# Adaptive condition and a feed-forward layer: the second half's condition product moved between the steps of the first group

## The reference

```python
W = weights[condition]                       # 32 of 16 matrices of 64 x 64, chosen by itok
y = einsum('bct,bcd->bdt', x, W)             # x: (32, 64, 1024)
h = gelu(einsum('bsd,df->bsf', y, inter_w) + inter_b, approximate=True)   # 1024 -> 4096
out = x + einsum('bsf,fd->bsd', h, output_w) + output_b                   # 4096 -> 1024
```

## Time and profile before

| | us |
|---|---|
| median of 3 runs (1282.69 to 1284.75) | 1283.48 |
| the profiled execution | 1285.43 |
| its span in the profile | 1282.4 |
| TensorE busy in it | 1258.2 |
| VectorE / ScalarE / GpSimd busy | 825.2 / 561.8 / 194.9 |
| granted TensorE clock, mean | 0.995 |

### The profile page before, as it was taken

How to read it: one execution, slowest core, us unless ns; L and a number is a source line. 1 busy time by engine, 2 the same in 40 slices (tenths; PEclk the granted TensorE clock), 3 DMA queues, 4 the chain that set the end, 5 groups by cost and what they waited for, 6 DMA issues and landing times.

```text
span 1282.4 us, 15344 instructions
## 1 busy us (share of the span) xinstructions
PE 1258.2 (98%) x5634; PEld 1043.3 (81%) x5634; DVE 825.2 (64%) x1078; ACT 561.8 (44%) x949; POOL 194.9 (15%) x105
## 2 busy tenths in 40 slices
PE   7799999999999999999999999999999999999998
PEld 7678888878888888888888888888888888888886
DVE  3857676877477677847665555554547767784764
ACT  3445544544454444444434444444445444444442
POOL 4623331223000000000033333222300000000000
PEclk9899999999999999999999999999999999999999
DMA  9625667654899433228735345443289942233431
GB/s 353 237 89 194 258 236 274 229 200 178 298 393 353 154 99 99 99 99 355 290 141 187 126 180 181 181 153 105 120 296 395 351 155 99 99 99 99 159 125 45
DMA packets 88601, 249.50 MB, mean 195 GB/s; under 512 B 8114, under 2 KB 8146, under 8 KB 87122
## 3 DMA queue, kind: packets, MB, share of 16 engines
q1 hardware_dynamic: 87442, 248.27, 53.3%
q10 hardware_dynamic: 1088, 0.28, 0.1%
HBM read 162.55 MB, written 85.98 MB: 194 GB/s over the span
## 4 chain that ended last, share of the span: by engine, by line
PE 91%; DVE 5%; DMA 3%; issue 1%; ACT 0%; SPq 0%; POOLq 0%; DVEq 0%; POOL 0%
PE ps L516 48%; PE ps L500 42%; DVE lhs L719 1%; PE ps L463 1%; DVE y L711 1%; DMA y_in<-y_raw_mem 1%; DMA h_mem<-c 1%; DMA y_raw_mem<-y_stage 1%; DVE y_whole L714 1%; DVE y_out L821 0%; DMA cond_all<-in_L_cond_weights_dram 0%; DVE y_stage L706 0%; DVE hs L733 0%; DVE y_whole L706 0%; DVE c L726 0%
## 5 line engine op out<-in xcount | busy, mean ns | idle before, releaser
L500 PE MATMUL ps<-y,lhs 128*128 128x512 f32 x2688 | 616.5, 391 | 10.5 <-DVE lhs L719 7.3
L516 PE MATMUL ps<-rhs,lhs 128*128 128x512 f32 x2688 | 609.6, 389 | 0.0
L500 PEld LDWEIGHTS ps<-y,lhs 128*128 128x128 f32 x2688 | 507.1, 189 | 119.5 <-issue 6.4
L516 PEld LDWEIGHTS ps<-rhs,lhs 128*128 128x128 f32 x2688 | 504.5, 188 | 104.8
L640 ACT ACTIVATE lhs<-h_raw 128x512 fp32r<-128x512 f32 x224 | 141.6, 632 | 345.8 <-PE ps L516 340.1
L778 DVE TENSOR_TENSOR lhs<-h_raw,lhs 128x512 fp32r<-128x512 f32 x224 | 155.1, 692 | 188.4 <-ACT lhs L640 188.4
L719 DVE TENSOR_TENSOR lhs<-w_raw,lhs 128x512 fp32r<-128x512 f32 x128 | 106.3, 831 | 132.1 <-ACT lhs L570 132.0
L719 DVE TENSOR_TENSOR lhs<-s_w,lhs 128x512 fp32r<-128x512 f32 x96 | 99.3, 1035 | 89.4 <-ACT lhs L570 89.3
L570 ACT ACTIVATE lhs<-w_raw 128x512 fp32r<-128x512 f32 x128 | 80.7, 632 | 172.1 <-PE ps L500 168.4
L781 DVE TENSOR_TENSOR rhs<-W,rhs 128x512 fp32r<-128x512 f32 x224 | 153.5, 685 | 0.0
L436 POOL TENSOR_TENSOR s_w<-w_raw 128x1024 f32<-128x1024 f32 x16 | 48.7, 3045 | 627.9 <-PE ps L516 354.6
(11 more groups left out here) (31 smaller groups left out, 287.7 us busy)
## 6 DMA issues: line engine op xcount, KB each, us to landing
h_raw<-h_mem SPq DMA_DIRECT2D x112, 512.0 KB, 3.4
w_raw<-in_L_ffn_inter_w_dram SPq DMA_DIRECT2D x32, 1024.0 KB, 9.0
h_mem<-hs SPq DMA_DIRECT2D x64, 512.0 KB, 4.9
W<-in_L_ffn_output_w_dram SPq DMA_DIRECT2D x32, 1024.0 KB, 12.7
h_mem<-c SPq DMA_DIRECT2D x48, 512.0 KB, 5.8
y_mem<-y_out SPq DMA_DIRECT2D x28, 512.0 KB, 3.1
y<-y_mem SPq DMA_DIRECT2D x7, 2048.0 KB, 13.6
x<-in_x_dram SPq DMA_DIRECT2D x16, 512.0 KB, 11.4
```

The lines of the kernel that those rows point to most:

```text
L500: last = nc.tensor.matmul(ps[:, bank, :], w[:, k, :], y[i][:, part, k, :], start=(i in FRESH and k == 0 and u == 0), stop=(k == KH - 1 and ...
L516: last = nc.tensor.matmul(ps[:, bank2(h, j, tb), :], lhs[s % RING][:, a, blk(tb)], rhs[r][:, w, :], start=(j in FRESH and q == 0 and u == ...
```

## The change

For the first pass `cond` is as before, tile by tile; its evictions are `y_keep`, `y_high`, `y_low` and `y_sum` work on halves of 1024 columns with a semaphore each, and steps 0 and 1 wait for the banks and halves that they use. The picks for these tiles are shared: GpSimd, ScalarE and VectorE each take every third, unrolled. The product of a tile of the second pass is a call of its own, `cond1(j)`. It writes two of the banks 4 to 7, and TensorE runs the eight of them behind steps 1, 1, 3, 3, 5, 5, 7 and 9 of group 0. Both evictions of a tile are ScalarE's (`y1_take`, three steps further on), into a staging buffer of 4 KiB used by every second tile, and SP stores them in two transfers with rows of 512 bytes. GpSimd makes the first four picks of these tiles before the weight sums of group 0 and the other twelve behind them; the sums wait only for the first half of the condition product. SP loads `w1` of group 0 behind the fourth x0 tile instead of the eighth, the last two x1 tiles when the first pass's product is done, `w1` of group 1 behind the store of the fifth tile, and b2 after all of them. The items have slots at c = 2, 4, ... 12 in groups 1 to 6, nine for each quarter, of which seven are used.

```diff
-        x1 = at("x1", 128, [TILES, D])
+        x1 = [at(f"x1_{j}", k, [D]) for j, k in enumerate((128, 132, 136, 140, 156, 216, 200, 184))]
...
-        y1_stage = [at(f"y1_stage{k}", 184 + 8 * k, [KH, BANK]) for k in range(2)]
+        y1_stage = [at(f"y1_stage{i}", 188 + 4 * i, [KB, P]) for i in range(2)]
...
-        def y1_item(g, i):
-
-
-            item = 5 * (g - 1) + i
-            return item if g > 0 and item < KH * PRODUCTS else None
+        def y1_item(g, c):
+
+
+
+            slot = 6 * (g - 1) + c // 2 - 1
+            kb, i = divmod(slot, PRODUCTS + 2)
+            return kb * PRODUCTS + i if 0 < g < NG - 1 and c in range(2, CHUNKS, 2) and i < PRODUCTS else None
+
+
+
+        BEHIND = (1, 1, 3, 3, 5, 5, 7, 9)
+
+        def pick(engine, i):
+
+            j, s = divmod(i, PER)
+            which = engine.value_load(itok_sb[0:1, i:i + 1], min_val=0, max_val=SETS - 1)
+            rows = slice(s * C, (s + 1) * C)
+            return wdiag[rows, j:j + 1, rows], cond_all[rows, bass.ds(which, 1), :]
...
             sp.dma_start(cond_all[0:C], cond_w.rearrange("s c d -> c s d")).then_inc(cond_in, 16)
             for j in range(TILES):
                 sp.dma_start(x0[:, j, :], x_tok[0, :, j, :]).then_inc(x0_in[j], 16)
-            load_w1(0, 0)
+                if j == TB - 1:
+                    load_w1(0, 0)
             for j in range(TILES):
-                sp.dma_start(x1[:, j, :], x_tok[1, :, j, :]).then_inc(x1_in[j], 16)
+                if j == TILES - 2:
+                    sp.wait_ge(cond_done, 2 * KB)
+                sp.dma_start(x1[j][:], x_tok[1, :, j, :]).then_inc(x1_in[j], 16)
+            for j in range(TILES):
+                sp.wait_ge(y1_taken, 2 * (j + 1))
+                n, cols = j // TB, blk(j % TB)
+                for k in range(2):
+                    sp.dma_start(y_raw_mem[:, :, 2 * k + n, cols].rearrange("k p t -> p k t"),
+                                 y1_stage[j % 2][:, k * KH:(k + 1) * KH, :]).then_inc(y1_staged[j % 2], 16)
+                if j == TB:
+                    load_w1(0, 1)
             sp.dma_start(b2_all[:], b2.partition_broadcast(P)).then_inc(b2_in, 16)
...
-                        for i in range(5):
-                            if y1_item(g, i) is not None:
-                                keep_y1(y1_item(g, i))
+                        for c in range(CHUNKS):
+                            if y1_item(g, c) is not None:
+                                keep_y1(y1_item(g, c))
...
+            for i in range(0, TILES * PER, 3):
+                to, of = pick(pool, i)
+                nc.gpsimd.tensor_copy(to, of).then_inc(picked[0], 1)
+            pool.wait_ge(picked[0], 6)
+
+            def picks1(first_j, end_j):
+                for i in range((TILES + first_j) * PER, (TILES + end_j) * PER):
+                    to, of = pick(pool, i)
+                    nc.gpsimd.tensor_copy(to, of).then_inc(picked1, 1)
+                pool.wait_ge(picked1, end_j * PER)
+
+            picks1(0, 2)
...
-                        pool.wait_ge(cond_done, 2 * KB)
+                        pool.wait_ge(cond_done, KB)
...
+                    if n == 0:
+                        pool.wait_ge(s_made[2], 1)
+                        picks1(2, TILES)
...
+            def cond(n):
                 for j in range(n * TB, (n + 1) * TB):
-                    pe.wait_ge((x0_in if h == 0 else x1_in)[j], 16)
-                    pe.wait_ge(wdiag_set, (h * TILES + j + 1) * PER)
+                    pe.wait_ge(x0_in[j], 16)
+                    for e in range(3):
+                        pe.wait_ge(picked[e], len(range(e, PER * (j + 1), 3)))
                     for kb in range(KB):
-                        if j == n * TB and r > 0:
-                            pe.wait_ge(y_odd if kb % 2 else y_even, (r - 1) * KB // 2 + kb // 2 + 1)
-                        last = nc.tensor.matmul(ps[:, kb, blk(j - n * TB)], tile[:, j, blk(kb)], wdiag[:, h * TILES + j, :],
+                        if j == TB:
+                            pe.wait_ge(kept_dve if kb % 2 else kept_act, kb // 2 + 1)
+                        last = nc.tensor.matmul(ps[:, kb, blk(j - n * TB)], x0[:, j, blk(kb)], wdiag[:, j, :],
                                                 start=True, stop=True)
                         if j == n * TB + TB - 1:
                             last.then_inc(cond_done, 1)
+
+            def cond1(j):
+
+                pe.wait_ge(x1_in[j], 16)
+                pe.wait_ge(picked1, PER * (j + 1))
+                if j < 2:
+                    pe.wait_ge(kept_act, KB)
+                    pe.wait_ge(kept_dve, KB)
+                else:
+                    pe.wait_ge(y1_taken, 2 * (j - 1))
+                for kb in range(KB):
+                    last = nc.tensor.matmul(ps[:, 4 + 2 * (j % 2) + kb // KH, blk(kb % KH)], x1[j][:, blk(kb)],
+                                            wdiag[:, TILES + j, :], start=True, stop=True)
+                    if kb % KH == KH - 1:
+                        last.then_inc(cond1_done, 1)
...
                 elif i == 0 and h > 0:
                     pe.wait_ge(acc_added, (PRODUCTS if g else PRODUCTS - 1) * 2)
                 elif i == 0 and g == 0:
-                    pe.wait_ge(y_even, 4 * KB // 2)
-                    pe.wait_ge(y_odd, 4 * KB // 2)
+                    pe.wait_ge(kept_dve if p else kept_act, KH + 1)
+                elif i == 0:
+                    pe.wait_ge(y1_taken, 2 * TILES)
+                if i == 1 and h == 0 and g == 0:
+                    pe.wait_ge(kept_dve if p else kept_act, KH + 2)
...
                 for k in range(KH):
+                    if (h, g, p) == (0, 0, 0) and k % 2 == 0:
+                        pe.wait_ge(y_split, 2 * i + k // 2 + 1)
...
+            for n in range(2):
+                cond(n)
             for h in range(PASSES):
                 for g in range(NG):
                     for c in range(CHUNKS):
                         first(h, g, c)
+                        if (h, g) == (0, 0):
+                            for j in range(TILES):
+                                if BEHIND[j] == c:
+                                    cond1(j)
...
+                    nc.scalar.activation(to[:, kb % KH, :], ps[:, kb, :], ACT.Copy).then_inc(kept_act, 1)
+
+            def y1_take(j):
+
+                for k in range(2):
+                    act.wait_ge(cond1_done, 2 * j + k + 1)
+                    if j >= 2 and k == 0:
+                        act.wait_ge(y1_staged[j % 2], 32 * (j // 2))
+                    nc.scalar.activation(y1_stage[j % 2][:, k * KH:(k + 1) * KH, :].rearrange("p k t -> p (k t)"),
+                                         ps[:, 4 + 2 * (j % 2) + k, :], ACT.Copy).then_inc(y1_taken, 1)
...
-            y_evict(0)
+            act.wait_ge(itok_in, 16)
+            act.wait_ge(cond_in, 32)
+            for i in range(1, TILES * PER, 3):
+                to, of = pick(act, i)
+                nc.scalar.activation(to, of, ACT.Copy).then_inc(picked[1], 1)
+            y_keep(0)
             y_high(0)
-            y_evict(1)
             high1(0, 0, 0)
             high1(0, 0, 1)
+            y_keep(1)
             y_high(1)
-            y_evict(2)
-            y_high(2)
-            y_evict(3)
             for h in range(PASSES):
                 for g in range(NG):
                     for c in range(CHUNKS):
                         if (h, g) != (0, 0) or c >= 2:
                             high1(h, g, c)
-                        if (h, g) == (0, 0) and 2 <= c < 6:
-                            y_high(c + 1)
+                        if (h, g) == (0, 0) and c in (3, 5, 7, 8, 10):
+                            y_high({3: 2, 5: 3, 7: 4, 8: 5, 10: 6}[c])
+                        if (h, g) == (0, 0):
+                            for j in range(TILES):
+                                if BEHIND[j] + 3 == c:
+                                    y1_take(j)
                         if g > 0:
                             trail(h, g - 1, c)
                         within(h, g, c)
-                        if h == 0 and c in (4, 6, 8, 10, 12) and y1_item(g, c // 2 - 2) is not None:
-                            y1_high(*divmod(y1_item(g, c // 2 - 2), PRODUCTS))
+                        if h == 0 and y1_item(g, c) is not None:
+                            y1_high(*divmod(y1_item(g, c), PRODUCTS))
...
+                for u in range(2):
+                    dve.wait_ge(y_hi, 2 * i + u + 1)
+                    half = slice(2 * u, 2 * u + 2)
+                    nc.vector.tensor_tensor(y[i][:, 1, half, :], whole[:, half, :], y[i][:, 0, half, :].bitcast(F32),
+                                            ALU.subtract).then_inc(y_split, 1)
...
-            y_evict(0)
+            dve.wait_ge(itok_in, 16)
+            dve.wait_ge(cond_in, 32)
+            for i in range(2, TILES * PER, 3):
+                to, of = pick(dve, i)
+                nc.vector.tensor_copy(to, of).then_inc(picked[2], 1)
```

(57 more changed lines are left out.)

71 lines of the change are left out of this document (23 added, 48 removed).

## The result

The changed kernel takes 1270.01 us (median; 1269.4 to 1270.38) beside 1283.59 for the kernel before, a ratio of 0.9893 with a 95% interval of 0.9876 to 0.991. The forecast was 1269.9. The profiled execution of the changed kernel took 1270.05, 1.8 over its span of 1268.2.

A forecast was written before the change was run, and what follows sets the result against it. TensorE, busy 1258.2 of 1282.4 us, was taken as the bound, so only its waits and slow-clock time could be won. 11.1 (group 0) plus 2.5 (items), 13.6 us, took 1283.48 to 1269.9; range 1264.5 to 1277.5.

The forecast's parts named there:

- Group 0, 11.1 us won: First group of pass 0: ends at 82.6 instead of 93.7 us, 11.1 us won.
- The chain: Opening of group 0: VectorE and GpSimd take turns by whole operations, putting step 0 at 27.8, step 2 at 38.5.
- The slow stretch of the clock: Step 0, behind 2.5 us of idleness: probably 1.2 GHz for 3 us, hidden under VectorE's chain.
- the 0.5 us before the third moved tile: Group 0, moved product: tile 2 waits 0.5 us for ScalarE's evictions behind y_high(2).
- The items, 2.5 us: Groups after group 0: new slots remove ScalarE's 5.69 us wait for y1_in, winning 2.5 us.
- Picks: Opening: picks shared by three engines, 1.03 us each taken, up to 3.4 free on ScalarE and VectorE.
- Loads: Opening: w1 of group 0 ahead of the last four x0 tiles; tile 4 waits half a microsecond.
- Staging: Staging buffers of the moved product, group 0: stores land in 5 us with 8.0 free, so cost zero.
- B: Group 0: turns cost nothing and TensorE alone bounds; 15.8 + 2.5 us won, 1265.2; chance 0.14.
- C: Opening: five VectorE operations each wait a pick cycle, a second slow stretch shows; 7.1 us less, 1277.0; chance 0.14.
- D: Group 0: the staging ring bounds, deciding from a 12.9 us landing; at 14, 1286.8 us; chance 0.04.
- E: Later groups: stalls stay, moved to the item at c=2; 11.1 us alone won, 1272.4; chance 0.10.

The follow-up runs named there:

- e2: The changed kernel with GpSimd's weight sums of group 0 started only when low1 of steps 0 and 1 is done: 1271.32 us, ratio 0.9904.
- e12: The changed kernel with GpSimd's sums of group 0 spread to where they are read, behind low1 of steps 1 and 3: 1267.14 us, ratio 0.9873.
- e1: The changed kernel with the items of the second 1024 put back to their old slots: 1273.45 us, ratio 0.9918.
- e7: The changed kernel with four extra stores per x1 tile to a scratch tensor, slowing the staging ring: 1291.44 us, ratio 1.0056.
- e10: The kernel before with GpSimd's weight sums of group 1 started only when low1 of step 8 is done: 1278.99 us, ratio 0.9963.
- e11: The changed kernel with the whole moved product ahead of step 0, w1 of group 1 behind all staging stores, its sums behind low1 of step 8: 1279.44 us.
- e4: The changed kernel with all 16 picks of the first 1024 on GpSimd: 1270.7 us, ratio 0.9895.
- e9: The changed kernel with w1 of group 0 loaded behind all eight x0 tiles again: 1271.86 us, ratio 0.9904.
- e8: The kernel before with the new slots of the items alone: 1281.46 us, ratio 0.9976.
- e13: e12 with w1 of group 0 loaded behind the sixth x0 tile instead of the fourth: 1266.08 us, ratio 0.9866.

## Why the prediction was right

*Group 0, 11.1 us won; measured 12.0.* The chain came out step for step: s1 at 17.7 (17.82), step 0 at 27.8 (27.43), step 2 at 38.5 (38.11), end at 82.6 (81.7), and e2 and e12 show that the turns it was made of are the cause. The first of these is in part luck: the forecast started s1 behind the product's first half (17.6), with `w1` landed at 16.8; in the trace that half ends at 16.94 and s1 waits for `w1`. Two terms were off. The slow stretch of the clock behind step 0's gap did not come. The gap was 1.46 and not 2.5, but that alone is not the reason: in e1 and e7 the same step came behind gaps of 2.16 and 2.61 and took 2.98 and 3.00, no slow step either. By the forecast's chain a slow stretch would have been hidden under VectorE's work. And the 0.5 us before the third moved tile did not come: ScalarE evicted in time.

*The last digit.* That 1269.9 and 1270.01 lie 0.1 apart is luck. The spans of the two profiled executions differ by 14.2 us, not by the 13.6 of the sum, and single runs of the kernel before lie up to 2 us apart (1282.69 to 1284.75).

*What the sum had only in its total.* The forecast read the 2.8 us `low1` of the old kernel as the price of turns in the opening, and used it there. That the same turns at 57 and 67 us made up 4.7 of the 12 us (6.2 by the profile) is in its figure of 93.7 against 82.6 but in none of its steps; e10 separates it. Nor did it count the turns that the later `w1` brings to 68 to 80 us: "TensorE bounds" held there although `low1` cost 2.29. By an estimate from e11 the place of the product is worth 1 to 2 us, so the forecast's picture of a product moved into gaps is the smaller part. The rest of the 12, some 4 to 6 us, came with the other parts together: halves, evictions on ScalarE, and the sums ahead of the second product. No run undoes one of these alone; the shared picks (e4) and the early `w1` of group 0 (e9) were undone and are worth nothing that the medians show.

*The items, 2.5 us; measured 2.1.* e8 gives the 2.5 in the old kernel; in the new one 0.44 is lost elsewhere, of which the gap of 0.20 before 106.67 is visible. ScalarE's wait for the store of the item at c = 2, put at 2 us, is there: four waits, 8.8 in all, the longest 3.11, none felt by TensorE. No wait for `y1_in` is left.

*Costs at nothing.* Picks: the two unknown engines need 0.65 (ScalarE) and 0.75 (VectorE) each, GpSimd 0.68 unrolled where the loop had 1.03; all under the 3.4 that was free. Loads: the wait before tile 4 was 1.61, not 0.5. x0 came at 18.56 rather than 18.1, but the product was there at 16.94 instead of 17.6; it cost nothing in this kernel, as e9 shows. Staging: the stores landed in 3.3 us (median; the longest 9.1) where 5 was taken, with 8 free, and ScalarE waited 0.3 for them in all; in e7 a buffer that came free after 8.1 cost nothing and one after 11.8 cost 2.61. `w1` of group 1 at 68.5 (70), `y1_in` at 81.8 (82.4).

*Rivals.* B (no turns) is refuted by the trace, and e12 and e13 show what it would have given: 1265.2 was its time, 1266.08 the measured time of a kernel in which no turn holds up a step. C needed a whole pick cycle for each VectorE operation; the picks cost them next to nothing (2.40 for two halves beside picks, 2.35 without). D needs a far slower ring than the 3.3 us here. E did not happen.

## What to carry to other kernels

Where GpSimd and VectorE both work on SBUF operands, look at who runs beside whom before moving matmuls: a sum that isn't needed for 20 us, started early because its data happens to be there, can cost the critical engine its full length several times over. Place such work beside VectorE's copies out of PSUM, or make it wait for a point at which VectorE has slack. When one edit moves several things, undo them singly. Here later sums of group 1 alone are worth 4.7 us (e10, in the kernel before), and in the change they come later only because a load was moved for want of memory; the step that gave the change its name is worth 1 to 2 by an estimate. And look at the clock behind a gap before adding up steps: in e11 a gap of 4.79 cost 7.5.

## What the runs showed of the hardware

The halves of `y_sum` and `y_low` beside the twelve picks (2.40 and 2.43 for two, against 2.35) show that short GpSimd copies of 0.23 hardly hold VectorE up; GpSimd waits instead (eight picks in 8.09 from 33.02, 1.01 each, where they take 0.68 without VectorE beside them).

Gaps of 2.67 and 3.79 us (e4, e9) were followed by a granted clock of 0.50, one of 2.73 (e2) by 1.00 and pairs of 5.72. Two gaps of 2.00 differ: the one in e10 was followed by full speed, the one before 70.44 in e8 by 0.50. The length of a gap alone doesn't tell. The product's first records are slow as well (64 records in 8.78 us, and the next 64 in 7.41), while the granted clock is shown as 1.00 there; no run shows why.
